# Fused cross-attention and quantised feed-forward block: denominators moved into a shared PSUM bank, a third bank for the row maxima, every order of work replaced

## The reference

```
def _L0_xattn_ref(q, k, v):          # q = layernorm(x), k = v = ctx
    qh = q.reshape(b * h, d // h, m)  # 8 heads of 32 rows, m = 512
    kh = k.reshape(b * h, d // h, -1)
    vh = v.reshape(b * h, c // h, -1)
    qk = einsum('bdm,bdn->bmn', qh, kh) * scale
    sm = softmax(qk, axis=-1)
    ret = einsum('bmn,bcn->bcm', sm, vh)

def _L0_ffn_ref(x, W1, W2):          # 512 -> 2048 -> 512
    h = silu(_bitlinear(x, W1))
    return _bitlinear(h, W2)

x = x + _L0_xattn_ref(_layernorm(x), ctx, ctx)
x = x + _L0_ffn_ref(_layernorm(x), W1, W2)
```

## Time and profile before

| | |
|---|---|
| median of 3 runs | 783.78 us (780.02 to 784.09) |
| span of the profiled execution | 780.7 us |
| own time of that execution | not given apart from its span |
| TensorE busy | 718.7 us, 92% |
| VectorE busy | 693.9 us, 89% |
| ScalarE busy | 634.8 us, 81% |
| GpSimd busy | 630.5 us, 81% |
| mean granted TensorE clock | 0.987 |

### The profile page before, as it was taken

The page is one execution under the profiler, slowest core; times in us unless marked ns, Lnnn a source line. Parts: engine busy times, 40 slices in busy tenths (PEclk is TensorE's granted clock), DMA queues, the critical chain, the costliest instruction groups (busy, mean ns, idle before and its releaser), DMA issues.

```text
span 780.7 us, 13868 instructions
## 1 busy us (share of the span) xinstructions
PE 718.7 (92%) x4324; PEld 280.2 (36%) x4324; DVE 693.9 (89%) x1588; ACT 634.8 (81%) x1017; POOL 630.5 (81%) x627
## 2 busy tenths in 40 slices
PE   0578699999999999999999999999999999999984
PEld 0112243333444444333344444333334344433322
DVE  2779999999999999999999999999999999997552
ACT  5486788888888898888888889888888888888852
POOL 3764778888889888888888998888888889877761
PEclk9999699999999999999999999999999999999998
DMA  8673213444333443344433334333443334330100
GB/s 293 167 197 111 55 43 107 109 110 109 98 92 84 109 99 78 96 109 109 109 101 92 85 105 100 81 92 109 110 109 103 94 86 101 82 82 25 46 28 13
DMA packets 53960, 76.66 MB, mean 98 GB/s; under 512 B 7808, under 2 KB 32384, under 8 KB 52864
## 3 DMA queue, kind: packets, MB, share of 16 engines
q1 hardware_dynamic: 53888, 75.79, 37.0%
HBM read 41.94 MB, written 8.39 MB: 64 GB/s over the span
## 4 chain that ended last, share of the span: by engine, by line
PE 83%; DVE 8%; DMA 3%; issue 2%; ACT 2%; SPq 1%; POOL 1%; POOLq 0%; ACTq 0%; DVEq 0%
PE pv L912 15%; PE mxp L902 15%; PE st L892 14%; PE bank_b L943 14%; PE dn L921 7%; PE bank_a L972 7%; PE bank_b L972 7%; DVE mx L727 4%; PE bank_a L931 3%; DMA late<-w 1%; DMA qs<-ql 1%; DMA qs<-qh 1%; ACT probs L585 1%; DVE late L796 1%; PE bank_a L954 1%
## 5 line engine op out<-in xcount | busy, mean ns | idle before, releaser
L585 ACT ACTIVATE probs<-st,sm 128x512 f32<-128x512 f32 x512 | 336.6, 687 | 52.7 <-PE st L892 26.9
L503 POOL TENSOR_TENSOR sums<-probs 128x512 f32<-128x512 f32 x256 | 333.3, 1321 | 20.8 <-ACT probs L585 20.8
L727 DVE TENSOR_REDUCE mx<-mxp 128x1 f32<-128x512 f32 x512 | 332.8, 676 | 18.5 <-PE mxp L902 14.9
L902 PE MATMUL mxp<-ks,qs 96*128 96x512 f16 x512 | 191.0, 403 | 18.2 <-DVE mx L727 12.4
L892 PE MATMUL st<-qs,ks 98*128 98x512 f16 x512 | 200.8, 394 | 1.7 <-ACT probs L585 1.6
L943 PE MATMUL bank_b<-w2t,late 128*128 128x512 f16 x512 | 128.1, 383 | 3.0 <-ACT late L615 3.0
L912 PE MATMUL pv<-probs,vt 128*32 128x512 f32 x1024 | 124.0, 602 | 0.0
L495 POOL TENSOR_TENSOR ql<-xn,qh 128x512 f16<-128x512 f32 x32 | 37.2, 1164 | 67.2 <-ACT qh L606 67.2
L892 PEld LDWEIGHTS st<-qs,ks 98*128 98x128 f16 x512 | 52.8, 103 | 99.3 <-ACT probs L585 40.1
L902 PEld LDWEIGHTS mxp<-ks,qs 96*128 96x128 f16 x512 | 50.7, 99 | 103.3 <-DVE mx L727 78.6
L801 DVE TENSOR_REDUCE hmx<-late 128x1 f32<-128x512 f32 x128 | 84.3, 679 | 1.1
(11 more groups left out here) (79 smaller groups left out, 896.6 us busy)
## 6 DMA issues: line engine op xcount, KB each, us to landing
cs<-ctx SPq DMA_DIRECT2D x32, 256.0 KB, 4.2
xs<-x SPq DMA_DIRECT2D x32, 256.0 KB, 4.0
late<-w SPq DMA_DIRECT2D x8, 1024.0 KB, 9.2
ks<-kh SPq DMA_DIRECT2D x64, 128.0 KB, 3.2
qs<-qh SPq DMA_DIRECT2D x64, 128.0 KB, 3.6
xr<-x SPq DMA_DIRECT2D x32, 256.0 KB, 3.0
vt<-values_t SPq DMA_DIRECT2D x32, 256.0 KB, 2.9
out<-late SPq DMA_DIRECT2D x32, 256.0 KB, 2.0
```

Of the source, the lines that this page charges most:

```text
L503: pool.tensor_tensor(sums[:, pair, h, :], probs[:, 2 * pair, h, :], probs[:, 2 * pair + 1, h, :], ALU.add).then_inc(sum_done, 1)
L585: act.activation(probs[:, c, h, :], st[u % 2][:, :], ACT.Exp, scale=sm1[:, r, ESC:ESC + 1]).then_inc(exp_done, 1)
L727: dve.reduce_max(mx[:, slot.ring(off), NC * h + c:NC * h + c + 1], mxp[m % 2][:, :], axis=AX.X).then_inc(max_done, 1)
L902: pe.matmul(mxp[m % 2][:, :], qs[0:3 * DH, r, h, c * P:(c + 1) * P], ks[0:3 * DH, r, h, :], start=True, stop=True).then_inc(mx_done, 1)
```

## The change

- The bank `dn` is gone. The denominators are summed in `bank_b`, and the inversion reads them there. `denominators` joins the users of `bank_b`: its first matmul waits for the gate of the chunk that had the bank before, and the next `second` waits for the inversion's transpose.
- `mxp` has three banks (`MXB = 3`). A maxima matmul waits for the read three before it. Banks are counted through over tiles.
- `weights_sum` uses `pv` instead of `bank_b`, and the first `values` waits for it.
- The bank waits are computed from the whole list of uses. `due` looks up a table; the loops run over more slots (-6 to TILES + 7), so that steps can be placed further ahead.
- All numbers of `PLAN`, `WEIGHTS` and `ORDER` are new.

```diff
+MXB = 3
+STB = 2
...
-    kh=[-38],
-    qh=[-30],
+    kh=[-43],
+    qh=[-47],
...
-    ql=[-33],
-    maxima=[-22, -22, -21, -20, -20, -18, -18, -14, -13, -12, -12, -11, -10, -9, -8, -7],
+    ql=[-48],
+    maxima=[-23, -22, -21, -20, -20, -20, -19, -18, -18, -13, -11, -11, -11, -9, -9, -9],
...
-    ct_low=[-5],
-    values=[17, 19, 19, 19],
-    sums=[4, 8, 9, 9, 10, 11, 11, 12],
+    ct_low=[-4],
+    values=[17, 19, 19, 20],
+    sums=[2, 6, 7, 8, 8, 8, 8, 8],
     denominators=[17, 17],
-    invert=[17],
-    attend=[20],
+    invert=[21],
+    attend=[23],
...
-    gate=[29, 30, 31, 32],
-    hidden_max=[29, 31, 32, 33],
+    gate=[29, 29, 31, 32],
+    hidden_max=[29, 29, 34, 34],
...
-    ht=[36, 39],
+    ht=[36, 38],
...
-    second=[38, 41, 41, 42],
-    finish=[45],
-    max_read=[-22, -21, -21, -20, -20, -18, -18, -13, -12, -11, -10, -10, -9, -8, -8, -8],
+    second=[38, 39, 40, 42],
+    finish=[48],
+    max_read=[-21, -20, -20, -20, -20, -20, -17, -13, -10, -9, -8, -8, -8, -6, -6, -6],
...
-    load=[-41],
-    load_v=[20],
-    stack_qh=[-19],
-    stack_kh=[-22],
-    stack_ql=[-14],
-    stack_kl=[-20],
-    xr=[6],
-    crow=[4],
-    store=[56],
+    load=[-36],
+    load_v=[46],
+    stack_qh=[-6],
+    stack_kh=[6],
+    stack_ql=[-1],
+    stack_kl=[2],
+    xr=[54],
+    crow=[27],
+    store=[101],
...
 WEIGHTS = dict(
-    load=[-36, -32, -30, -27, -2, 3, 7, 18],
+    load=[-79, -70, -55, -22, 15, 25, 30, 38],
...
-    quantise=[-25, -20, -15, -7, 12, 15, 21, 23],
+    quantise=[-31, -25, -23, -21, 15, 15, 16, 30],
...
-        mxp = [pb(f"mxp{k}", [P, D], f32) for k in range(2)]
+        mxp = [pb(f"mxp{k}", [P, D], f32) for k in range(MXB)]
         pv = pb("pv", [P, D], f32)
-        dn = pb("dn", [P, D], f32)
...
+        BANK_B = users(("denominators", 0, dn_spread, 1, 1), ("first", 0, gate_done, FC, 1), ("first", 2, gate_done, FC, 3),
+                       ("second", 0, y_scaled, 1, 1))
...
-                dve.transpose(dspread[:, :, :].rearrange("p a b -> p (a b)"), dn[:, :]).then_inc(dn_spread, 1)
+                dve.transpose(dspread[:, :, :].rearrange("p a b -> p (a b)"), bank_b[:, :]).then_inc(dn_spread, 1)
...
-                wait(pe, max_done, slot, UNITS, off, m - 1)
-                pe.matmul(mxp[m % 2][:, :], qs[0:3 * DH, r, h, c * P:(c + 1) * P], ks[0:3 * DH, r, h, :],
+                wait(pe, max_done, slot, UNITS, off, m + 1 - MXB)
+                pe.matmul(mxp[slot.at(UNITS, off, m) % MXB][:, :], qs[0:3 * DH, r, h, c * P:(c + 1) * P], ks[0:3 * DH, r, h, :],
...
                 if pair == 0:
-                    wait(pe, dn_spread, slot, 1, off - 1, 1)
+                    bank_free(pe, BANK_B, slot, off, "denominators", 0)
                 for h in range(TH):
-                    last = pe.matmul(dn[DH * h:DH * (h + 1), :], ones[:, 0:DH], sums[:, pair, h, :],
+                    last = pe.matmul(bank_b[DH * h:DH * (h + 1), :], ones[:, 0:DH], sums[:, pair, h, :],
```

More of the change, by code:

```diff
@@ L108 @@
-    rows=[-44, -32, -16, -7],
-    abs=[-32, -30, -24, -18, -8, -3, 8, 11],
-    sum=[-23, 12],
-    quantise=[-25, -20, -15, -7, 12, 15, 21, 23],
-    convert=[-13, -9, -6, 4, 18, 21, 22, 24],
-)
[L117 to L125, removed]
@@ L128, in due @@
-def due(u, step):
-    return [(-(at // UNITS), (n,) if len(PLAN[step]) > 1 else ())
-            for n, at in enumerate(PLAN[step]) if at % UNITS == u]
+    load=[-79, -70, -55, -22, 15, 25, 30, 38],
+    rows=[-80, -2, -67, -22],
+    abs=[-46, -41, -33, -30, -12, -1, 7, 11],
+    sum=[-28, 14],
+    sum_pe=[-25, 13],
+    quantise=[-31, -25, -23, -21, 15, 15, 16, 30],
+    convert=[-25, -17, -8, -1, 18, 18, 23, 33],
+)
+ORDER = {
+    'pool': ['finish', 'quantise', 'xn', 'ql', 'xn2', 'sums', 'residual', 'hidden_quantise',
+        'key_rsqrt', 'rstd', 'rstd2'],
+    'act': ['kh', 'tanh', 'qh', 'ct_evac', 'quantise_act', 'key_squares', 'ht_evac', 'rescale',
+        'xqt_evac'],
+    'dve': ['absmax2', 'key_scale_b', 'norm2', 'invert_c', 'gate', 'aggregate', 'invert_b',
+        'norm2b', 'hidden_max', 'hidden_scale_d', 'hidden_scale', 'scale2', 'scale2_b', 'ct_low',
+        'max_read', 'hidden_scale_c', 'key_scale', 'invert', 'attend', 'moments', 'stats_x', 'kl',
+        'moments2', 'hidden_scale_b'],
+    'pe': ['key_norm', 'maxima', 'first', 'ht', 'xqt', 'second', 'values', 'denominators', 'ct'],
+    'sp': ['stack_ql', 'stack_qh', 'load_v', 'store', 'load', 'xr', 'crow', 'stack_kh', 'stack_kl'],
+}
@@ L412, in run @@
                     for name in ORDER["sp"]:
[L413 to L415 removed]
+                        for off, number in due(slot, u, name):
+                            steps[name](slot, off, *number)
                     for at, step, *which in weights:
@@ L428, in _, with users, bank_free @@
                 sp.wait_ge(y_stored[r], 16 * (TILES // 2 + 1))
[L431 to L455, removed]
+        def users(*steps):
+            order = sorted((position(step, n, t), ORDER["pe"].index(step), -t, n, step, done, per_tile * t + m)
+                           for step, n, done, per_tile, m in steps for t in range(TILES))
+            return {(step, n, -t): (before[5], before[6]) for before, (_, _, t, n, step, _, _) in zip(order, order[1:])}
+        BANK_A = users(("key_norm", 0, key_clamped, 1, 1), ("ht", 0, ht_evac, 2, 1), ("ht", 1, ht_evac, 2, 2),
+                       ("ct", 0, ct_low, 1, 1), ("xqt", 0, xqt_evac, 1, 1),
+                       ("first", 1, gate_done, FC, 2), ("first", 3, gate_done, FC, 4))
+        BANK_B = users(("denominators", 0, dn_spread, 1, 1), ("first", 0, gate_done, FC, 1), ("first", 2, gate_done, FC, 3),
+                       ("second", 0, y_scaled, 1, 1))
+        def bank_free(engine, users, slot, off, step, n=0):
+            if (step, n, slot.b + off) in users:
+                engine.wait_ge(*users[step, n, slot.b + off])
         @block.gpsimd
@@ L969, in first @@
                     wait(pe, xqt_evac, slot, 1, off, 1)
-                bank_free(pe, users, slot, off, place("first", fc))
+                bank_free(pe, before, slot, off, "first", fc)
                 for j in range(NC):
@@ L976, in weights_sum @@
                 pe.wait_ge(w_step, WS * k + 1)
-                pe.matmul(bank_b[:, 0:1], ones[:, :], wst[:, k, 4:5], start=True, stop=True).then_inc(w_sum, 1)
-            weights = [(WEIGHTS["sum"][k], weights_sum, k) for k in range(2)]
+                pe.matmul(pv[:, 0:1], ones[:, :], wst[:, k, 4:5], start=True, stop=True).then_inc(w_sum, 1)
+            weights = [(WEIGHTS["sum_pe"][k], weights_sum, k) for k in range(2)]
             def run(slot):
```

123 lines of the change are left out of this document (66 added, 57 removed).

## The result

The changed kernel took 795.24 us in the median of four runs (793.41 to 796.29), the kernel before 783.75 in four runs of the same comparison. The ratio is 1.0163, its 95% interval 1.0134 to 1.0192: slower by 1.6%, three times the 0.5% that the prediction took a measurement to tell. The forecast was 775.0 with a range of 764 to 786; it failed, and on the wrong side.

What follows compares the result with a forecast made beforehand. The prediction took TensorE to bound a steady tile, 0.6 us of it due to the banks, and VectorE the start; 4 us from tiles plus 5 from the start gave 783.8 - 9 = 775 us, range 764 to 786.

Steps and rivals of the forecast that it cites:

- other moves: Remaining re-placements (POOL's `finish`, `xn` and `ql`, SP's store and residual loads): each has units of slack, taken as 0.
- Third maxima bank, and the stall of 0.30 us that stays: Steady tile, TensorE: a third bank removes up to 0.60 us of waits for reads; 0.30 remains at maxima 5.
- Steady tile 21.48: Tile time forecast from 21.63 - 0.60 + 0.19 + 0.30 = 21.52, taken as 21.48; 4 us gained in all.
- Denominators in `bank_b` at 0: Denominators' new wait for the third chunk's gate: it ends some 1.0 us before their turn, so cost 0.
- The rule of rotating banks: Independent matmul groups rotate through PSUM banks; by it alone the denominators' gate is uncovered and the time above before.
- The rival of the late values' load: SyncE issues the values' load later; landing beyond 4.2 us delays TensorE every tile: about 791 us, chance 0.09.
- Slower than before, at 791 and 794: Two slower rivals: late values' load, 791 us, chance 0.09; denominators waiting for the gate, 794 us, chance 0.06.
- Start, 5 us: Earlier loads recover 7 of VectorE's 9.9 us idle, maxima begin 2 us later: net 5 us gained, ends -2 and +8.
- Tail, 0: After the last maxima: `attend` of tile 31 0.5 us later, earlier second gate gives about 0.4 back; taken as 0.
- The mark set for tile 1: Sign of the faster start: values of tile 1 at 96 to 99 us instead of 102.9.

Runs made afterwards that it cites:

- Number 5: Changed kernel with `kl` ahead of three maxima reads it had followed, `ct_low` and two reads a unit earlier; 777.64 us, ratio 0.9955 to the kernel before.
- Number 4: Separate small kernel: VectorE and GpSimd operations of this kernel's shapes, alone and side by side; `kl` 0.78 us each alone, 1.55 beside two-input additions.
- number 3: Kernel before with the new banks (third maxima bank, denominators in `bank_b`) but its old `PLAN`, `WEIGHTS` and `ORDER`; 777.72 us, ratio 0.9947.

## Why the prediction was wrong

**The step that failed** is the price of `kl` at its new place, in the part on the denominators. The prediction entered it as 0.67 us ("0.2, five reads, 0.67 for `kl`, four operations of 0.60") and so placed the gate of the third chunk 6.3 us after `ct_low`. From the start of `kl` to that of the first gate it is 1.65 us (290.99 to 292.64), and the third chunk's gate starts 7.36 us after `ct_low` (287.80 to 295.16). For the denominators, which the prediction asked about, this did no harm: TensorE was late by then, too. But by the same terms the first chunk's gate was due 3.9 us after `ct_low`, and it started at 4.84. For that gate the third chunk's matmuls wait, in the kernel before as in the changed one, and the sum has no term for this wait: it fell under "other moves", taken as 0. It had the 0.2 us to spare that were found above, and cost 0.78 us a tile. The prediction even had a row of a VectorE operation drawn out beside GpSimd, the weight clamp of 2.17 us in the earlier trace rows, and used it only to say that the clamps cost the same either way. Number 5 settles it: `kl` elsewhere, nearly all other new orders kept, and the tile is 21.45 against 21.48 forecast.

That a row's duration holds for the neighbours it was taken beside is the lesson, and it could have been seen: where the kernel before starts `kl`, 0.19 us ahead of a sum, that sum has 1.68 us instead of 1.26. The Trainium skill (SBUF — State Buffer, Who interferes with whom) says that a VectorE instruction with two SBUF inputs contends with a GpSimd instruction that reads SBUF, that one with at most one SBUF input doesn't unless it runs in a two-port mode, and that the order of issue decides who is held, and then wholly. Number 4 agrees in its numbers on the inputs: 1.55 against 0.78 us with two in SBUF, 0.72 with one of them in PSUM. On the order the recorded starts agree where they lie 0.14 us or more apart and both operations are of full size, and not always below that (number 5). Whether the other is held wholly the traces can't tell, as the recorded times overlap a little (the pair's time, below).

**The rest, point by point.**

- *Third maxima bank, and the stall of 0.30 us that stays:* right. Weight loads wait 0.67 us a tile (forecast under 1) in the changed kernel and 1.03 in number 5, the stall is 0.23 and 0.30.
- *Steady tile 21.48:* wrong as a whole (22.15); right without the collision (21.45).
- *Denominators in `bank_b` at 0:* right. They waited for a gate once, 2.7 us, in the whole run, and not at all in number 3. The rule of rotating banks that the prediction drew from the Trainium skill (Perfetto Trace Analysis, Matmuls), and by which the gate would have stood uncovered, decided nothing here. Yet a gate did decide, that of a chunk that had shared this bank before the change.
- *The rival of the late values' load:* its premise came true, its price did not. In ten tiles the load landed in 4.2 to 4.8 us, over the stated 4.2, and yet no matmul waited for it; the load had more room than worked out, and not only since the tile was longer: in number 5, with its tile of 21.45, the matmuls don't wait for it either.
- *Slower than before, at 791 and 794:* the size was met (795.2) by luck, the mechanisms were not. The 0.15 on the slower side was too little: five engines in 16 units of 1.35 us, everything re-ordered, and "other moves: 0" in one line is where a price with two ends was missing.
- *Start, 5 us:* mis-sized, it gave 2.0, and even that is not clearly the start's new order, since number 3 gained 2.4 with the old one. The maxima began at 26, as said. But of 7 us of idle time only 2.4 came back: the keys of tile 2 are still issued behind the maxima rows of tile 0 and two loads, and landed at 55.6 after 9.14 us, where the prediction had counted on the queries alone. From 62.7 us on the chain runs over VectorE, with three of the four W2 clamps (six operations, 10.2 us) ahead of the inversion of tile 0 and the fourth (3.4 us) ahead of that of tile 1. The mark set for tile 1, 3.9 to 6.9 us earlier than before, was missed: its `attend` came 2.0 us earlier.
- *Tail, 0:* the changed kernel lost 1.0 us after the last `attend`, number 5 gained 0.5 there (29.5 against 30.0). Why was not tried.

With `kl` in its harmless place the profile of number 5 divides like this against that of before: 2.0 us in the start, 3.7 in the tiles (the forecast's 4), 0.5 in the tail; its span is 774.5 against 780.7. The medians differ by less, 3.9 us.

## What to carry to other kernels

A duration taken from a trace is that of an instruction and its neighbours. When a change moves an operation of VectorE with two inputs in SBUF, look in the same microsecond at what GpSimd does; if it has just begun a long operation on SBUF, price the moved one by what is left of the other plus 0.55 us (this `kl`; its own 0.74 alone), and prefer a place beside nothing, or where it starts 0.2 us ahead: starts within 0.13 us of each other fell out either way. Other forms may be held as well, as the clamp with its single SBUF input was; look at the spread of an operation's durations in the trace, where 0.741 in the median and 2.381 at most were already on record. When engines grow busier with the same instructions, compare the mean of each form before reading any wait: the culprit stands as busy, and the wait it makes is put down to the innocent step behind it.

## What was not expected of the hardware

- A start 0.09 us behind GpSimd's made an operation of 0.74 us take 1.73, in every steady tile and to within 0.02 us the same. In number 4 an addition and a `kl` side by side follow each other every 1.67 us, less than the 0.75 and 1.26 us that they last alone in sum. So the recorded times overlap; of a held `kl` 0.19 us do, as it ends 0.55 us after the addition and takes 0.74 alone. Whether work overlaps there or only the starting of an instruction isn't shown.
- GpSimd operations with one SBUF input hold `kl` up too. They are shorter, 0.62 us alone, so it is held less (1.01 against 0.78 us); it ends 0.54 us after them, as after an addition. And even an operation of GpSimd on a single column is drawn out by `kl`, from 0.55 to 1.27 us.
- Sharing the denominators' bank with two chunks and `second` was free, while the third maxima bank, the aim of 0.60 us of stalls, gave 0.09 a tile with the old orders. A wait of the weight loads for ScalarE's copy, 0.7 us a tile, stands where theirs for the reads was.
